# Last expert of a mixture-of-experts kernel: bias products on GpSimd, cross products in a bank of their own, a tile's scale moved up

## The reference

```python
logits = x_flat @ router_w + router_b
gates = softmax(logits)                     # each token goes to its 2 best experts
buf = ...                                   # (8, 640, 256): the tokens of each expert
h = gelu(einsum('ecd,edh->ech', buf, w1) + b1)       # hidden width 1024
out = einsum('ech,ehd->ecd', h, w2) + b2             # back to 256
y = einsum('ned,ne->nd', gathered, gates * valid)    # sum over a token's experts
x = layernorm(x + y)
```

## Time and profile before

| | us |
|---|---|
| median of 3 runs | 926.44 |
| lowest and highest | 926.04, 926.61 |
| the profiled execution | 922.29 |
| its span, first to last instruction | 920.5 |
| TensorE busy | 884.7 (96%) |
| VectorE busy | 640.0 (70%) |
| ScalarE busy | 730.0 (79%) |
| GpSimd busy | 486.2 (53%) |
| a `prepare` of VectorE in the last expert, mean of 5 | 0.483 |
| TensorE, tiles of the last expert, 901.5 to 916.0 | 9.34 of 14.5 |
| VectorE, same stretch | 12.98 of 14.5 |
| GpSimd, same stretch | 7.81 of 14.5 |

### The profile page before, as it was taken

How to read it: one execution, slowest core, us unless ns; L and a number is a source line. 1 busy time by engine, 2 the same in 40 slices (tenths; PEclk the granted TensorE clock), 3 DMA queues, 4 the chain that set the end, 5 groups by cost and what they waited for, 6 DMA issues and landing times.

```text
span 920.5 us, 19382 instructions
## 1 busy us (share of the span) xinstructions
PE 884.7 (96%) x7317; PEld 501.6 (54%) x7317; DVE 640.0 (70%) x1187; ACT 730.0 (79%) x892; POOL 486.2 (53%) x408
## 2 busy tenths in 40 slices
PE   7999999999999999999999999999589999999995
PEld 5434344434334444434443443334489999998994
DVE  5788556547886655888666577527657877888787
ACT  5688978897797899789789879998365787778864
POOL 2489245246475645646664454541513566666665
PEclk9999999999999999999999999999799999999998
DMA  5644467643436345253433524622261745534411
GB/s 167 163 127 150 143 215 223 217 167 111 159 135 223 116 134 215 79 201 138 164 110 112 194 98 170 204 64 84 79 213 37 254 137 179 172 115 132 156 61 66
DMA packets 62504, 135.40 MB, mean 147 GB/s; under 512 B 10558, under 2 KB 31398, under 8 KB 62272
## 3 DMA queue, kind: packets, MB, share of 16 engines
q1 hardware_dynamic: 41936, 72.88, 24.6%
q0 software_dynamic: 20464, 61.18, 19.1%
HBM read 69.20 MB, written 62.35 MB: 143 GB/s over the span
## 4 chain that ended last, share of the span: by engine, by line
PE 81%; DVE 11%; DMA 3%; issue 3%; POOL 2%; ACT 0%; SPq 0%; DVEq 0%; POOLq 0%
PE opsum L1028 24%; PE spsum L1004 23%; PE hp L1701 12%; PE yp L1667 5%; PE misc L860 4%; PE yp L1677 3%; PE misc L903 3%; PE misc L873 2%; DMA out<-eo,add_idx 2%; DVE oden L1418 1%; PE misc L864 1%; POOL others L1588 1%; PE tp L1655 1%; DVE emb L1217 1%; DMA res<-in_xT 1%
## 5 line engine op out<-in xcount | busy, mean ns | idle before, releaser
L800 ACT ACTIVATE prob<-spsum 128x1024 f32<-128x1024 f32 x512 | 493.4, 1022 | 85.8 <-PE spsum L1004 81.5
L1028 PE MATMUL opsum<-prob,val 128*17 128x512 f32 x2048 | 270.5, 598 | 2.8 <-DVE oraw L1410 2.1
L1004 PEld LDWEIGHTS spsum<-stacks 32*128 32x128 f32 x1536 | 73.5, 183 | 113.0 <-ACT prob L800 61.7
L1004 PEld LDWEIGHTS spsum<-area_q 32*128 32x128 f32 x1536 | 72.6, 183 | 112.2 <-ACT prob L800 65.2
L1004 PE MATMUL spsum<-stacks 32*128 32x512 f32 x1536 | 133.0, 425 | 0.4 <-issue 0.4
L1004 PE MATMUL spsum<-area_q 32*128 32x512 f32 x1536 | 131.9, 425 | 1.0 <-ACT prob L800 0.9
L1418 DVE RECIPROCAL oden<-oden 128x256 f32<-128x256 f32 x62 | 108.7, 1753 | 2.1
L681 POOL TENSOR_TENSOR onorm<-oraw,oden 128x512 f32<-128x512 f32 x31 | 42.1, 1358 | 98.6 <-DVE oden L1418 98.5
L595 POOL TENSOR_TENSOR area_s<-emb,area_s 128x1024 fp32r<-128x1024 f32 x28 | 66.6, 2378 | 45.9 <-DVE area_s L1225 45.9
L1028 PEld LDWEIGHTS opsum<-prob,val 128*17 128x17 f32 x2048 | 36.1, 95 | 88.6 <-ACT prob L800 51.3
L593 POOL TENSOR_TENSOR square<-raw 128x512 bf16<-128x512 f32 x28 | 52.0, 1857 | 57.2 <-DVE raw L1205 57.1
(11 more groups left out here) (262 smaller groups left out, 1379.1 us busy)
## 6 DMA issues: line engine op xcount, KB each, us to landing
split_scratch<-area_s POOLq DMA_DIRECT2D x56, 512.0 KB, 4.1
area_k<-in_w SPq DMA_DIRECT2D x16, 1024.0 KB, 5.8
area_q<-split_scratch SPq DMA_DIRECT2D x28, 512.0 KB, 5.5
stacks<-split_scratch SPq DMA_DIRECT2D x24, 512.0 KB, 5.4
rows<-dispatched SPq DMA_DIRECT2D x7, 662.5 KB, 4.9
aT<-onorm SPq DMA_DIRECT2D x124, 32.0 KB
staged<-in_xT SPq DMA_DIRECT2D x7, 512.0 KB, 4.2
dispatched<-last_rows POOLq DMA_DIRECT2D x2, 1722.5 KB, 14.2
```

The source lines that it names most:

```text
L800: act.activation(prob[u % NPB][:], spsum[u % NSB][:].rearrange("p a n -> p (a n)"), ACT.Exp, scale=HD ** -0.5).then_inc(s_exp, 1)
L1004: ins = pe.matmul(spsum[u % NSB][:, j % 2, :], kst[par][rows, a, P * kt:P * (kt + 1)], qst[par][rows, b, cols], start=i == 0, stop=i == 2 ...
L1028: ins = pe.matmul(opsum[32 * j:32 * j + HD + 1, :], val[b % 2][:, kt, h0 + j, :], prob[(2 * s + j // 2) % NPB][:, HALF * (j % 2):HALF * (j ...
```

## The change

All of it is in the last expert.

Bias products on GpSimd: VectorE's `prepare` goes for expert 7. In its place GpSimd's `biased_sums(t)` multiplies b2 by the gate into the free tile `rows`, waits for itself and for the tile's gather, and adds the product to `others`. For t = 0, 1, 2 it stands behind the gathers 2, 3 and 4, for t = 3 and 4 behind the last output store of expert 5. VectorE waits for s_biased ahead of each first combination.

Cross products in a bank of their own: for tiles 1 to 4 the two cross products (high hidden by low weights, low hidden by high weights) are summed in the bank tp, 16 products of 256 columns, ahead of the 8 main products of 256 columns in yp. TensorE signals the cross sum by s_half, and VectorE's first combination waits for that, its second for s_y. Tile 0 is made as before, except that the first four products of tile 1 that stand within it are cross products now. The main sum no longer holds a low part; the cross sum holds both. Nothing of the reference is left out.

Fourth tile's scale: `finish_tile(3)` on VectorE and `normalise` of tile 3 on ScalarE stand behind the statistics of tile 3, and no longer behind those of tile 4.

```diff
@@ block.gpsimd
+            def biased_sums(t):
+
+                bias = rows[LAST % 2][:, t, 0:DIM]
+                if t == 0:
+                    pool.wait_ge(s_bias, 16)
+                    pool.wait_ge(s_turned, ST * EXPERTS)
+                pool.tensor_scalar(bias, b2[:, LAST, :], gate[LAST % 2][:, t:t + 1], None, ALU.mult
+                                   ).then_inc(s_poolchain, 1)
+                pool.wait_ge(s_poolchain, t + 1)
+                pool.wait_ge(s_gather[t], 16 * LAST)
+                pool.tensor_tensor(others[:, t, :], bias, others[:, t, :], ALU.add).then_inc(s_biased, 1)
...
                 for t in range(ST if e else 0):
                     pool.wait_ge(s_h, HK * e + 3 + t)
                     gather_sums(e, t)
+                    if e == LAST and t >= 2:
+                        biased_sums(t - 2)
                 if e >= 2:
                     pool.wait_ge(s_h, HK * (e + 1))
                     store_outputs(e - 2, 4)
+                if e == LAST:
+                    for t in range(ST - 2, ST):
+                        biased_sums(t)
@@ block.tensor
+            def cross_products(t, i, first, end):
+
+                n = ST * LAST + t
+                if first == 0 and i == 0:
+                    pe.wait_ge(s_z, n - 1)
+                for m in range(first, end):
+                    ins = pe.matmul(tp[n % 2][:, 0:DIM], hids[:, i, m, P * t:P * (t + 1)],
+                                    w2s[LAST % 2][:, 1 - i, m, :], start=i == 0 and m == 0,
+                                    stop=i == 1 and m == HK - 1)
+                if i == 1:
+                    ins.then_inc(s_half, 1)
+
+            def main_products(t):
+
+                n = ST * LAST + t
+                for m in range(HK):
+                    ins = pe.matmul(yp[n % 2][:, 0:DIM], hids[:, 0, m, P * t:P * (t + 1)],
+                                    w2s[LAST % 2][:, 0, m, :], start=m == 0, stop=m == HK - 1)
+                ins.then_inc(s_y, 1)
...
-                        high_part(e, 1, 0, HK // 2)
+                        if e == LAST:
+                            cross_products(1, 0, 0, HK // 2)
+                        else:
+                            high_part(e, 1, 0, HK // 2)
                         high_part(e, 0, HK - 1, HK)
                         low_part(e, 0, HK - 1, HK)
+                    elif e == LAST:
+                        cross_products(t, 0, HK // 2 if t == 1 else 0, HK)
+                        cross_products(t, 1, 0, HK)
+                        main_products(t)
@@ block.scalar
             for t in range(ST):
                 rstd_guess(LAST + t, LAST, slice(t, t + 1))
-                if t:
+                if t and t < ST - 1:
                     normalise(LAST + t - 1, LAST, (t - 1,))
+                if t == ST - 2:
+                    normalise(LAST + t, LAST, (t,))
@@ block.vector
-                dve.wait_ge(s_y, n + 1)
-                link(dve.scalar_tensor_tensor(others[:, t, :], yp[n % 2][:, DIM:2 * DIM], g, others[:, t, :],
-                                              ALU.mult, ALU.add))
+                if e == LAST:
+                    dve.wait_ge(s_biased, t + 1)
+                if e == LAST and t:
+                    dve.wait_ge(s_half, t)
+                else:
+                    dve.wait_ge(s_y, n + 1)
+                cross = tp[n % 2][:, 0:DIM] if e == LAST and t else yp[n % 2][:, DIM:2 * DIM]
+                link(dve.scalar_tensor_tensor(others[:, t, :], cross, g, others[:, t, :], ALU.mult, ALU.add))
+                if e == LAST and t:
+                    dve.wait_ge(s_y, n + 1)
...
-                    if e == LAST and m >= HK - 3:
-                        prepare(e, m - (HK - 3))
...
                         tell_variances(LAST + t, e, slice(t, t + 1))
-                        if t + 3 < ST:
-                            prepare(e, t + 3)
-                        if t:
+                        if t and t < ST - 1:
                             finish_tile(e, t - 1)
+                        if t == ST - 2:
+                            finish_tile(e, t)
             finish_tile(LAST, ST - 1)
```

More of the change, by code:

```diff
@@ L1538, in experts @@
         s_var, s_rstd, s_shift, s_final = sem("s_var2"), sem("s_rstd2"), sem("s_shift"), sem("s_final")
-        s_tail = sem("s_tail")
+        s_tail, s_half, s_biased, s_poolchain = sem("s_tail"), sem("s_half"), sem("s_biased"), sem("s_poolchain")
         s_chain, s_actchain = sem("s_chain2"), sem("s_actchain2")
```

## The result

| | before | after |
|---|---|---|
| median of 5 runs, us | 926.61 | 932.44 |
| lowest and highest | 926.04, 928.41 | 931.43, 934.55 |
| ratio, with its 95% interval | 1 | 1.006 (1.0043 to 1.0077) |
| the profiled execution | 922.29 | 932.44 |
| its span | 920.5 | 930.6 |

The changed kernel is slower by 5.8 us, 0.6%. The two profiled executions are not alike ahead of the change: 4.2 us of the 10.1 us between their spans have passed before the last expert's hidden layer is done, in code that is the same. So from here on I count from the end of the last product of L1738 (L1701 before), 900.7 in this trace, and call the rest the tail. It grew by 5.9 us, about as much as the medians did (5.8).

A forecast was written before the change was run, and what follows sets the result against it. GpSimd's queue was taken to bound the last expert: five pairs ahead of the stores move the final one 4.9 us later. Added to the profiled 922.29 that is 927.2, on the median 926.44 it is 931.4 us; range 929.0 to 934.6.

The forecast's parts named there:

- last store, by the queue alone: The final output store, when GpSimd's queue is free for it: at 922.60 us against 917.68, 4.9 us later.
- last store, by VectorE: The final output store, if only VectorE's chain held it: VectorE done at 920.33, plus 0.79, giving 921.12 us.
- The pair's price: One bias product and sum on GpSimd: 0.04 + 0.93 + 0.08 + 0.70 = 1.75 us, from 1.67 to 2.39.
- The queue: GpSimd's gathers, five pairs and stores in the last expert: pairs ahead of the stores delay the final one by 4.9 us.
- VectorE's slack of 1.5 us: At the end of the last expert, VectorE's path would be ready 1.5 us before GpSimd is free for the final store.
- the half clock: TensorE after idling, at tile 2: 2.9 us at half clock, costing VectorE 0.3 of its 1.5 us slack.
- My own test for this: Ahead of the final store: an idle GpSimd would mean VectorE or TensorE was slower and the 1.5 us slack absent.
- The moved scale: Fourth tile's scale directly behind its statistics: tile 4 loses cover, leaving VectorE a 0.46 us exposed wait for ScalarE.
- The cross bank: TensorE's cross products in their own bank: 2.82 us a tile against 2.81, cost nothing.
- Rival A: VectorE's three subtractions block GpSimd's pairs, adding 2.5 us ahead of expert 5's store: 933.9 us; chance 0.12.
- Rival B: TensorE stays at half clock to the end after idling: last store at 928.0, time 936.8 us; chance 0.04.
- Rival C: The GpSimd pair costs little, so the kernel isn't slower: 926.5 us; chance 0.08.

The follow-up runs named there:

- e0: The changed kernel run again unchanged, on another chip: 926.17 us, ratio 1.0059 to the kernel before.
- e3: The changed kernel with all five pairs (bias product and sum) behind expert 5's last output store: 925.00 us, ratio 1.0047 to the kernel before.
- e6: e3 with each bias product made twice on GpSimd, the extra one into a free tile: 930.90 us, ratio 1.011 to the kernel before.
- e7: e2 with the pairs of tiles 3 and 4 on GpSimd, in its two idle stretches: 921.60 us, ratio 1.0008 to the kernel before.
- e2: The changed kernel without the pairs, VectorE preparing as before; cross bank and moved scale kept: 921.31 us, ratio 1.0002 to the kernel before.
- e11: The changed kernel run a third time, unchanged: 932.13 us, ratio 1.0065 to the kernel before.
- e1: The kernel before with only the bias pairs moved to GpSimd; cross products and scale as before: 928.33 us, ratio 1.0083 to the kernel before.
- e5: The changed kernel with the fourth tile's scale back behind the fifth's statistics: 926.51 us, ratio 1.0052 to the kernel before.

## Why the prediction was right

It said 931.4 us, slower, in a range from 929.0 to 934.6; measured were 932.4. Step by step:

| step | predicted | after | e0 |
|---|---|---|---|
| store of expert 5 starts | 7.14 | 7.34 | 7.35 |
| VectorE released | 9.95 | 9.60 | 9.60 |
| first store of expert 6 | 12.41 | 12.10 | 12.10 |
| first store of expert 7 | 20.94 | 20.58 | 20.58 |
| last store, by the queue alone | 26.06 | 25.69 | 25.69 |
| last store, by VectorE | 24.58 | 27.09 | 26.50 |

All are in us from the end of the hidden layer's products (896.54 in the prediction's sums).

**The pair's price** held. Two pairs with nothing beside them stand at 909.20 and 910.92, 1.72 us apart, against 1.75: product 0.93 as taken, sum 0.73 against 0.70. In e3, e6 and e7 the sum is 0.64 or 0.72 to 0.74.

**The queue** held in mechanism and size, shown by e2 (no pairs, no loss), e3 and e6. It is 0.4 us shorter than the sum, because the transfers between and behind the pairs took GpSimd 1.09 to 1.30 us where the sum has 1.43 to 1.47 (below). VectorE's release is early for the same reason: the store of expert 5 took 1.09 us instead of 1.64, and so it was 2.26 us from its start to VectorE's, not 2.81.

**VectorE's slack of 1.5 us** is the step that failed. I had it end ahead of the queue; it ended 1.4 us behind it. One term was too small, and one wait stood nowhere in the sum. I gave the half clock 2.9 us and a loss of 0.3; it lasted 3.0 us in after and cost 0.45, but 5.3 in e0, where VectorE's waits for TensorE add up to 1.7 us. And no row of before had a late signal, which took 1.9 us in after. A small term was off too: from VectorE's last instruction to the last store it is 0.99 us, not 0.79. My own test for this stood in the prediction, an idle GpSimd ahead of the final store, and it came up. The two errors, -0.37 for the queue and +1.40 for VectorE behind it, are together the 1.0 us between 931.4 and 932.4. That they have opposite signs is luck, and so is a part of the closeness of the number.

**The moved scale**: predicted exposed wait 0.46 us, measured 0.57 (925.75). **The cross bank**: cost nothing, as said; tile 3 took 2.81 us, and e2 the time of before. That it would gain something beside the pairs I had not said.

**Rival A**, the engines blocking each other, is real but small. Beside VectorE's subtraction a product took 1.59 us instead of 0.93, the next 1.20, and the subtraction 1.33 instead of 0.83. That is 0.9 us on GpSimd ahead of the store, not the rival's 2.5. All three subtractions met an instruction of a pair: the first cost GpSimd 0.66 us, in the second it was VectorE that paid (0.50 us), and the third, already half over, cost GpSimd 0.27. The Trainium skill, "SBUF — State Buffer", section "Who interferes with whom", has it that the instruction issued second is blocked in full. The small instructions agree with that (e7's at 899.72 ends with GpSimd's sum); the large ones agree only in part: the product that started with a subtraction at 898.89 ended 0.72 us behind it (899.76 to 900.48), less than the 0.93 that it takes by itself. **Rival B** fell: full clock was back by the start of tile 3 in after, e0 and e11 (at 914.35, 912.93 and 916.79). **Rival C** fell with the measured pair, and e6 shows that the queue charges each product in full.

## What to carry to other kernels

Before work is moved to an engine because it is idle on average, look at where its queue has transfers that others wait for: here 53% busy left no room ahead of the stores that the end waits for, and five pairs of 1.7 us on GpSimd cost 5 us, and spared VectorE two exposed instructions of 0.48. Where a chain is held by a queue, count every instruction ahead of the last transfer and check whether the second path ends close behind: a slack of 1.5 us in one trace was not one in the next.

## What the runs showed of the hardware that I had not expected

- An indirect transfer on GpSimd took 1.43 to 1.64 us with 0.30 us ahead of it in the hidden layer, and 1.09 to 1.30 with 0.15 to 0.35 directly behind a computation (901.65, 905.07 and 908.05 in after). This gave back most of what the engines' blocking took. It need not be the computation ahead that does it: in the tail a store behind another store takes 0.97 with 0.30 ahead, the same 1.27 us in all. What sets the slow ones apart is what VectorE does beside them. From 700 us on in the trace of before, the 7 stores with at least 0.4 us of a subtraction (L1934) beside them have a median of 1.47 us, the 38 with neither a subtraction nor a bias product beside them 0.97. No run changed this alone.
- TensorE's half clock behind about 5 us of idle time lasted 3.0 us of products in after, and 4.6 to 5.3 in e0, e1, e5 and e11.
- On some chips signals of TensorE come up to 3.1 us behind the start of the product that gives them, where 0.3 is usual, and VectorE then stands idle for 0.5 to 2.2 us.
